# Product-key layer: the scatter matmuls of two token halves of 64 rows become one of 128 rows with block-diagonal moving columns

## What is computed

```python
q = (xn @ w_q.T).reshape(b, n, 2, h, kd).transpose(2, 0, 1, 3, 4)   # h = 8 heads, kd = 128
sim = jnp.einsum('pbnhd,hkpd->pbnhk', q, keys)                      # nk = 64 keys on each side
s, i = jax.lax.top_k(sim, k)                                        # k = 8
all_scores = (sx[..., :, None] + sy[..., None, :]).reshape(b, n, h, k * k)
all_idx = (ix[..., :, None] * nk + iy[..., None, :]).reshape(b, n, h, k * k)
scores, pk = jax.lax.top_k(all_scores, k)
idx = jnp.take_along_axis(all_idx, pk, axis=-1)                     # 64 of 4096 rows for each token
o = jnp.einsum('bnd,bnhkd->bnhk', inputs, key_in[idx])
o = jax.nn.gelu(o, approximate=False) * jax.nn.softmax(scores, axis=-1)
return jnp.einsum('bnhk,bnhkd->bnd', o, key_out[idx])
```

## Time and profile before

| | us |
|---|---|
| median of 3 runs | 3340.21 (3339.08 to 3341.33) |
| the profiled execution | 3339.34 |
| its span in the profile | 3337.5 |
| PE busy | 3087.6 |
| DVE busy | 1924.5 |

### The profile page before, as it was taken

How to read it: one execution, slowest core, us unless ns; L and a number is a source line. 1 busy time by engine, 2 the same in 40 slices (tenths; PEclk the granted TensorE clock), 3 DMA queues, 4 the chain that set the end, 5 groups by cost and what they waited for, 6 DMA issues and landing times.

```text
span 3337.5 us, 72505 instructions
## 1 busy us (share of the span) xinstructions
PE 3087.6 (93%) x28718; PEld 2424.1 (73%) x28718; DVE 1924.5 (58%) x6590; ACT 1239.6 (37%) x2763; POOL 445.7 (13%) x417
## 2 busy tenths in 40 slices
PE   7999869999999999999999999956898966999997
PEld 5578568777777777777777777624666645999996
DVE  3245457666666666666666666525666635444443
ACT  0133222333333333333333333223666642555553
POOL 0366000000000000000000000002222211333332
PEclk9999969999999999999999999967999986999998
DMA  3122430101011110101010110110122112222223
GB/s 131 43 87 87 150 130 5 33 18 33 19 32 28 22 30 21 33 17 33 17 33 19 32 28 22 31 27 20 56 84 75 43 49 86 39 36 39 36 39 77
DMA packets 89665, 153.50 MB, mean 46 GB/s; under 512 B 17152, under 2 KB 72192, under 8 KB 86176
## 3 DMA queue, kind: packets, MB, share of 16 engines
q1 hardware_dynamic: 68736, 111.50, 11.8%
q0 software_dynamic: 20448, 37.32, 5.3%
q10 hardware_dynamic: 144, 0.03, 0.0%
HBM read 100.53 MB, written 52.46 MB: 46 GB/s over the span
## 4 chain that ended last, share of the span: by engine, by line
PE 74%; DVE 5%; ACT 3%; DMA 2%; issue 2%; SPq 1%; POOL 0%; POOLq 0%; DVEq 0%; ACTq 0%
PE ps L847 14%; PE ps L670 13%; PE ps L830 8%; PE ps L908 8%; PE ps L1779 8%; PE ps L1794 7%; PE ps L881 3%; PE ps L698 2%; PE ps L699 2%; PE ps L1242 1%; PE ps L1307 1%; PE ps L1184 1%; PE ps L1286 1%; PE ps L1358 1%; DMA arena<-in_kout 1%
## 5 line engine op out<-in xcount | busy, mean ns | idle before, releaser
L670 PEld LDWEIGHTS ps<-arena 128*128 128x128 f32 x4096 | 536.9, 192 | 29.7 <-issue 2.5
L847 PE MATMUL ps<-arena 128*128 128x256 f32 x2048 | 551.4, 393 | 0.0
L670 PE MATMUL ps<-arena 128*128 128x128 f32 x4096 | 539.7, 276 | 1.9 <-ACT arena L678 1.9
L847 PEld LDWEIGHTS ps<-arena 128*128 128x128 f32 x2048 | 355.3, 190 | 161.6 <-issue 132.1
L678 ACT ACTIVATE arena<-ps 128x256 f32<-128x256 f32 x512 | 192.8, 383 | 527.4 <-PE ps L670 526.6
L929 DVE SCALAR_TENSOR_TENSOR arena<-arena 128x128 f32<-128x128 f32 x256 | 74.0, 289 | 451.4 <-ACT arena L920 451.3
L908 PE MATMUL ps<-arena 128*16 128x256 f32 x4096 | 284.1, 397 | 37.8 <-DVE arena L938 37.4
L830 PE MATMUL ps<-arena 64*128 64x32 f16 x8192 | 296.7, 245 | 1.7 <-DVE arena L818 1.7
L920 ACT ACTIVATE arena<-ps 128x256 f32<-128x256 f32 x256 | 97.6, 381 | 538.9 <-PE ps L908 538.9
L830 PEld LDWEIGHTS ps<-arena 64*128 64x128 f16 x8192 | 277.1, 157 | 18.1 <-DVE arena L818 2.7
L1779 PE MATMUL ps<-arena 128*128 128x128 f32 x2272 | 267.3, 276 | 0.7 <-DVE arena L1851 0.7
(11 more groups left out here) (272 smaller groups left out, 4833.4 us busy)
## 6 DMA issues: line engine op xcount, KB each, us to landing
xw_scratch<-arena SPq DMA_DIRECT2D x32, 512.0 KB, 2.6
arena<-xw_scratch SPq DMA_DIRECT2D x128, 128.0 KB, 4.3
arena<-in_W SPq DMA_DIRECT2D x16, 1024.0 KB, 5.3
arena<-ys_scratch SPq DMA_DIRECT2D x16, 512.0 KB, 8.8
x_scratch<-arena SPq DMA_DIRECT2D x64, 128.0 KB, 2.0
xn_scratch<-arena SPq DMA_DIRECT2D x32, 129.0 KB, 2.7
arena<-in_xT SPq DMA_DIRECT2D x8, 512.0 KB, 8.0
arena<-in_kinT SPq DMA_DIRECT2D x1, 4096.0 KB, 14.5
```

Of the source, the lines that this page charges most:

```text
L670: m = e.matmul(bank(b)[:, 128 * i:128 * i + 128], kin[:, k, 2 * jp + i, :], xcT[:, k, 128 * blk:128 * blk + 128], start=(k == 0), stop=(k ...
L847: m = e.matmul(bank(7)[:, 0:256], G[blk % 2][:, j, :], kout[:, j, :], start=(j == 0), stop=(j == 31))
```

## The change

The two matmuls of a token's halves become one. Its 128 rows of `X` are the stationary operand, and its moving operand has 64 columns: 32 for the first half's token and 32 for the second half's. The first 32 are zero on partitions 64 to 127 and the other 32 on partitions 0 to 63, because the weights with which DVE multiplies are zero there. For this `R16` is filled so that the weight stands in plane 0 on the lower partitions and in plane 3 on the upper, a new array `L16` does the same for the low part, and both are set to zero once. `Y12` doubles, the fine one-hot gets an array `Y1` of its own, which both multiplies of DVE read with a broadcast dimension, and some small arrays move. A group's PSUM layout changes from half, token, column to token, half, column.

```diff
-        Y12 = [take(2, 32, 16, dt=f16) for _ in range(2)]
+        Y1 = take(32, 16, dt=f16)
+        Y12 = [take(2, 2 * 32 * 16, dt=f16).rearrange("p i (v j q) -> p i v j q", v=2, j=32) for _ in range(2)]
...
-            e.activation(R16[64:128, 0:3], tp[64:128, :, 64:128], ACT.Copy).then_inc(s["zr"], 1)
+            e.activation(R16[64:128, 1:4], tp[64:128, :, 64:128], ACT.Copy).then_inc(s["zr"], 1)
...
-            e.tensor_tensor(R16[0:64, 3], tp[0:64, 2, 0:64], R16[0:64, 2], ALU.subtract)
-            e.tensor_tensor(R16[64:128, 3], tp[64:128, 2, 64:128], R16[64:128, 2], ALU.subtract).then_inc(s["zv"], 1)
+            e.tensor_tensor(L16[0:64, 0], tp[0:64, 0, 0:64], R16[0:64, 0], ALU.subtract)
+            e.tensor_tensor(L16[64:128, 1], tp[64:128, 2, 64:128], R16[64:128, 3], ALU.subtract).then_inc(s["zv"], 1)
...
+            if n:
+                e.wait_ge(s["xy"], 3 * n)
...
-            e.tensor_tensor(Y12[b][:, 1], iot[:, 0:32], R16[:, 1, t0:t0 + 16].unsqueeze(1).to_broadcast([128, 32, 16]),
+            e.tensor_tensor(Y1, iot[:, 0:32], R16[:, 2, t0:t0 + 16].unsqueeze(1).to_broadcast([128, 32, 16]),
                             ALU.is_equal).then_inc(s["xy"], 1)
-            e.tensor_tensor(X[b], iot, R16[:, 0, t0:t0 + 16].unsqueeze(1).to_broadcast([128, 128, 16]), ALU.is_equal)
+            e.tensor_tensor(X[b], iot, R16[:, 1, t0:t0 + 16].unsqueeze(1).to_broadcast([128, 128, 16]), ALU.is_equal)
             e.wait_ge(s["xy"], 3 * n + 1)
-            e.tensor_tensor(Y12[b][:, 0], Y12[b][:, 1], R16[:, 2, t0:t0 + 16].unsqueeze(1).to_broadcast([128, 32, 16]),
-                            ALU.mult).then_inc(s["xy"], 1)
-            e.wait_ge(s["xy"], 3 * n + 2)
-            e.tensor_tensor(Y12[b][:, 1], Y12[b][:, 1], R16[:, 3, t0:t0 + 16].unsqueeze(1).to_broadcast([128, 32, 16]),
-                            ALU.mult).then_inc(s["xy"], 1)
+            for i, w in ((0, R16[:, 0:4:3, t0:t0 + 16]), (1, L16[:, :, t0:t0 + 16])):
+                e.tensor_tensor(Y12[b][:, i], Y1.unsqueeze(1).to_broadcast([128, 2, 32, 16]),
+                                w.unsqueeze(2).to_broadcast([128, 2, 32, 16]), ALU.mult).then_inc(s["xy"], 1)
...
                 for i in range(2):
-                    for half in range(2):
-                        p0 = 64 * half
-                        m = e.matmul(bank(4 + half)[:, 32 * q:32 * q + 32], X[b][p0:p0 + 64, :, q],
-                                     Y12[b][p0:p0 + 64, i, :, q], start=(i == 0), stop=(i == 1))
+                    m = e.matmul(bank(4, 2)[:, 64 * q:64 * q + 64], X[b][:, :, q],
+                                 Y12[b][:, i].rearrange("p v j q -> p (v j) q")[:, :, q], start=(i == 0), stop=(i == 1))
...
-            e.tensor_tensor(gv, gv, bank(4, 2).rearrange("p (g t j) -> p g j t", g=2, j=32), ALU.mult).then_inc(s["A"], 1)
+            e.tensor_tensor(gv, gv, bank(4, 2).rearrange("p (t g j) -> p g j t", g=2, j=32), ALU.mult).then_inc(s["A"], 1)
...
+            e.memset(R16, 0.0)
+            e.memset(L16, 0.0)
```

More of the change, by code:

```diff
@@ L583, in build @@
         h0 = take(2, 16)
+        assert arena.at <= WORDS - 2496
         Wx4 = Wx.rearrange("p k (g f u) -> p (k g) f u", g=4, f=4)
@@ L639, in build @@
         X = [take(128, 16, dt=f16) for _ in range(2)]
-        Y12 = [take(2, 32, 16, dt=f16) for _ in range(2)]
-        pr, eq, io8k = take(8, 8, 8), take(16, 64, dt=f16), take(8, 64, dt=f16)
+        Y1 = take(32, 16, dt=f16)
+        Y12 = [take(2, 2 * 32 * 16, dt=f16).rearrange("p i (v j q) -> p i v j q", v=2, j=32) for _ in range(2)]
+        pr, io8k = take(8, 8, 8), take(8, 64, dt=f16)
+        eq = take_at(arena.at - 768, 16, 64, dt=f16)
         xn = take(2, 128)
@@ L644, in build @@
         sc, pk = take(8, 8), take(8, 8, dt=u32)
-        ab, abf = take(2, 64, dt=u32), take(2, 64, dt=f16)
-        ixy = take(2, 64)
+        ab, abf = take_at(WORDS - 2496, 2, 64, dt=u32), take_at(WORDS - 2368, 2, 64, dt=f16)
+        ixy = take_at(WORDS - 256, 2, 64)
         ge, es, ss = take(64), take(8, 8), take(8)
         Z = take(3, 2, 64)
-        R16 = take(4, 64, dt=f16)
+        R16, L16 = take(4, 64, dt=f16), take(2, 64, dt=f16)
         xr = take(2, 256)
@@ L652, in build @@
         xWn, xWl = take(1024), take(8, 256)
-        th, hs_ = take(64), take(64)
+        th, hs_ = take_at(WORDS - 128, 64), take_at(WORDS - 64, 64)
         gtc, mm2 = take_at(route_at, 320), take_at(route_at + 320, 128)
@@ L659, in build, with z_ab @@
         gate_ps = bank(6)[:, 0:256]
+        def z_ab(at_):
+            return Z.rearrange("p a b c -> p (a b c)")[:, at_:at_ + 128].rearrange("p (d r) -> p d r", d=2)
         def dup(v):
@@ L768, in rows_vector @@
                 e.wait_ge(s["z_tr"], blk)
-            e.scalar_tensor_tensor(Z[:, 0], dup(ixy[:, 0]), 2.0, dup(ge), ALU.mult, ALU.add).then_inc(tk, 1)
+            e.scalar_tensor_tensor(z_ab(64), dup(ixy[:, 0]), 2.0, dup(ge), ALU.mult, ALU.add).then_inc(tk, 1)
             e.wait_ge(tk, k + 15)
             e.reciprocal(ss, ss).then_inc(tk, 1)
-            e.scalar_tensor_tensor(Z[:, 1], dup(ge), -32.0, dup(ixy[:, 1]), ALU.mult, ALU.add).then_inc(tk, 1)
+            e.scalar_tensor_tensor(z_ab(192), dup(ge), -32.0, dup(ixy[:, 1]), ALU.mult, ALU.add).then_inc(tk, 1)
             e.wait_ge(tk, k + 17)
@@ L775, in rows_vector @@
             e.wait_ge(tk, k + 19)
-            e.tensor_copy(Z[:, 2].rearrange("p d (k h) -> p d k h", k=8),
+            zf = Z.rearrange("p a b c -> p (a b c)")
+            e.tensor_copy(zf.rearrange("p (x r) -> p x r", r=64)[:, 0:6:5].rearrange("p d (k h) -> p d k h", k=8),
                           es.rearrange("p h k -> p k h").unsqueeze(1).to_broadcast([128, 2, 8, 8])).then_inc(tk, 1)
```

## The result

The changed kernel takes 3710.8 us in the median of 4 runs (3706.34 to 3710.87) against 3339.64 us for the kernel before beside it; the ratio is 1.1109, with a 95% interval of 1.109 to 1.1128. That is 371 us more. The forecast was 3657 us in a range of 3535 to 3775.

What follows compares the result with a forecast made beforehand. The prediction took PE to bound the kernel: 3339.3 us + 221 for streaming columns + 96 for the clock = 3656, and 3657 us with the median 0.9 us above the profiled execution; range 3535 to 3775 us.

Steps and rivals of the forecast that it cites:

- PE is the bound without slack: Product-key stage: PE busy 1608.71 of 1610 us, so each scatter group's added cost is paid for nearly all 128 groups.
- Moving columns, not instructions: Scatter matmuls: time is streaming of strided moving columns at about 1.8 ns each, not a price for each instruction.
- 124 ns: New 64-column scatter matmul, from a line through 67 ns at 32 columns and 267 at 144; 221 us more in all.
- The change of shape: Around a scatter group: 0.10 us at entry falls away, an estimated 0.10 us at exit into the LSTM step stays.
- The clock: Product-key stage: granted clock falls to 0.50 in 64 of 128 groups, 1.5 us each, 96 us.
- DVE and PSUM: Multiplies grow to 0.68 us, the wider PSUM read costs at most 4.7 us a block; DVE stays under PE.
- Instructions as the price: Rival, scatter matmuls: 33 ns for a load and its matmul whatever they stream, 3190 us; chance 0.05.
- free steps: Rival, scatter matmuls: the step costs nothing at 64 columns, a matmul takes 56 ns, 3281 us; chance 0.04.
- loads alone: Rival, scatter matmuls: the weight load sets the pace at 67 ns, -13 us, 3327 us; chance 0.04.
- a fixed 267 ns: Rival, scatter matmuls: a strided 128-row matmul costs 267 ns whatever its columns, 806 us more, 4146 us; chance 0.04.
- the clock falls in nearly every group: Rival, product-key stage: 96 to 128 clock falls, columns at 124 to 128 ns, 3705 to 3775 us; chance 0.13.
- the forecast case: Scatter groups: matmuls at 119 to 128 ns, clock falls in a quarter to three quarters, 3590 to 3705 us; chance 0.45.

Runs made afterwards that it cites:

- the split group: Changed kernel with each scatter group in two parts of 8 tokens, ahead of and behind the output and gelu matmuls: 3604.7 us against 3371.3 for the kernel before.
- weights packed: Changed kernel with the 128 stationary columns read packed, moving ones still 16 elements apart (wrong numbers): 3653.8 us against 3371.3 for the kernel before.
- step 8: Changed kernel with moving columns read 8 elements (16 bytes) apart in place of 16 (wrong numbers): 3744.2 us against 3339.6 for the kernel before.

## Why the prediction was right, step by step

- *PE is the bound without slack.* Right: PE is busy for 1970.00 of 1970 us in the stage of the changed kernel, and what a group takes more came out at the end (for the split group, 221 us by the timeline and 233 us of device time in one run).
- *Moving columns, not instructions.* Right, and shown from both sides: half the columns with the same instructions halve a matmul (66 ns), and half the instructions with nothing strided gain nothing (1.03 us against 0.90 and 0.10 for the entry).
- *124 ns.* Right in size (125 measured) and only partly in its reason. The line went through the 67 ns of a pair as if that were columns alone, and there it was lucky. It is the larger of 59 ns for columns and 61 for loads, with some 5 on top. The 267 ns of L171 were the sound end: at 64 columns 1.83 ns a column, and 8 ns more beside a strided load, are the 125. One row was misread: the x16 in rows 6 counts the L171 matmuls that touch a stretch, not those that start in it. In each of the first two stretches, one at either clock, 14 start, so the conclusion stands.
- *The change of shape.* Right: 0.89 us ahead of a group, and 4.11 us with the exit, where I had 4.07.
- *The clock.* The mechanism was right, with its price near and its count too low. I took 64 falls at 1.5 us, 96 us; the 64 were half of all groups, a choice between none and all and not worked out from a row. Measured are 365 us at 0.50, which is 107 times 3.4 us in 87 stretches, and 145 us lost, 1.36 for each 3.4 us. This is the term that was mis-sized, and it makes up nearly all of the 54 us between forecast and result. In 20 of the 87 cases it lasts twice as long (1434 to 1440.8 around the first group shown), which the forecast didn't have at all.
- *DVE and PSUM.* 0.68 us as said; the wider step in PSUM costs nothing.
- *Rivals.* Instructions as the price (3190 us), free steps (3281), loads alone (3327) and a fixed 267 ns (4146) are all ruled out. The result lies at the lower edge of "the clock falls in nearly every group" (3705 to 3775), which I had given 0.13, next to the forecast case. By their own terms the upper ends are 3722 us for the forecast case (128 ns, 96 falls) and 3770 for its neighbour (128 ns, 128 falls), in place of the 3705 and 3775 that I wrote. So the result lies where the two touch: 87 groups with a fall are within the forecast case's quarter to three quarters, and the time at 0.50, worth 107 falls, is not.

## What to carry to other kernels

Before packing two matmuls into one with zeros, find out what a matmul costs there: divide the start-to-start time by its moving columns and compare with another matmul of the trace that has another number of columns, and keep in mind that the weight load may stand close behind (59 ns for columns and 61 for the load in the 67 ns of a pair here). If the columns are the price, block-diagonal packing doubles it, while two half-height matmuls in different rows of the array already run side by side. Look at the step in bytes between the columns of both operands before the count of instructions: bringing neighbours within a line of 16 bytes, without giving up a last dimension that steps by one on DVE, was worth 4.0% here, and the change that halved the instructions cost 11%.

## What the runs showed of the hardware

- The strided f16 moving operand of TensorE cost about 1.9 ns for each 16-byte line it touched: 1.83 ns a column with steps of 32 bytes, 121/64 = 1.89 with 16, 65/64 = 1.0 at most with 8. The load of 128 strided weights took 61 ns, a quarter of that price for each column; why a quarter isn't shown. For the moving columns the price is the same at both clocks: in the changed kernel a scatter matmul takes 125 ns on average at 1.00 and 126 at 0.50, and L171 of the kernel before 267 and 268.
- Packed, 64-row matmuls with their loads follow each other at 12.6 ns, and 128-row ones with 64 columns at 29 ns.
- In the changed kernel the granted clock fell from 1.00 to 0.50 beside the scatter groups 87 times, and PE was busy for all of the 1970 us from 510 to 2480. Each of these stretches began 2.8 to 4.8 us after the first matmul of a group of 4.11 us; with the same matmuls in two parts of 2 us and 1.8 us of f32 matmuls between them, it fell twice. How often it falls isn't settled by the length of the group alone. Groups of 3.86 us (weights packed) had 61 stretches and 212 us at 0.50, groups of 3.98 us (step 8) had 114 and 461 us, and groups of 4.11 us had 87 and 365 us. The price was alike in all three: 88, 195 and 145 us in this order over what the streaming explains, 0.40 to 0.42 us for each us at 0.50. Why it is not 0.5 is open but for the part of a stretch that lies in the scatter group itself, 27 of the 365 us.
- On DVE an f16 operand repeated along the last dimension nearly doubles the time (2281 against 1215 ns), and a last dimension of only 4 neighbours does not (1216 ns).
